# Another order of loads, scatters and VectorE's work in the up half of a fused projection and expert feed-forward kernel

## The reference

```python
ys = y * scale
d = rsqrt(einsum('bi,io->bo', ys * ys, weight * weight) + EPS)
xf = einsum('bsi,io->bso', x * ys[:, None, :], weight) * d[:, None, :]     # 512 -> 512
top1 = argmax(softmax(xf @ gate_w.T))                                       # 2 experts
masked = xf[None] * one_hot(top1, 2).T[:, :, None]
h = relu(einsum('end,edh->enh', masked, w1) + b1[:, None, :])               # 512 -> 2048
routing_output = (einsum('enh,ehd->end', h, w2) + b2[:, None, :]).sum(axis=0)
shared = relu(xf @ sw1 + sb1) @ sw2 + sb2                                   # 512 -> 2048 -> 512
out = x + routing_output + shared
```

## Time and profile before

| | |
|---|---|
| Time, median of 3 runs | 1463.98 us (1463.56 to 1464.52) |
| Time of the profiled execution | 1463.63 us |
| Its span in the profile | 1460.7 us |
| TensorE's mean granted clock | 0.993 |
| TensorE busy (matmuls) | 1425.5 us, 98% |
| TensorE, weight loads | 1175.8 us, 80% |
| VectorE busy | 847.2 us, 58% |
| ScalarE busy | 501.4 us, 34% |
| GpSimd busy | 314.4 us, 22% |
| HBM traffic over the span | 149 GB/s |

### The profile page before, as it was taken

How to read it: one execution, slowest core, us unless ns; L and a number is a source line. 1 busy time by engine, 2 the same in 40 slices (tenths; PEclk the granted TensorE clock), 3 DMA queues, 4 the chain that set the end, 5 groups by cost and what they waited for, 6 DMA issues and landing times.

```text
span 1460.7 us, 17708 instructions
## 1 busy us (share of the span) xinstructions
PE 1425.5 (98%) x6262; PEld 1175.8 (80%) x6262; DVE 847.2 (58%) x1362; ACT 501.4 (34%) x776; POOL 314.4 (22%) x354
## 2 busy tenths in 40 slices
PE   9997999999999999999999999999999999999998
PEld 8776778877877888888888888888888888888886
DVE  7895887857777878777864514224245532423235
ACT  4453553535454444444533211111123221111112
POOL 0000000062132110000023240614215151340533
PEclk9999899999999999999999999999999999999999
DMA  6947548494778898977675220312106231120312
GB/s 207 248 159 201 216 177 238 167 260 173 242 263 279 277 298 261 287 256 233 214 214 169 60 50 11 66 20 47 39 14 201 60 62 26 29 57 2 66 22 33
DMA packets 157190, 215.66 MB, mean 148 GB/s; under 512 B 46560, under 2 KB 67552, under 8 KB 157120
## 3 DMA queue, kind: packets, MB, share of 16 engines
q1 hardware_dynamic: 142240, 186.71, 39.9%
q0 software_dynamic: 14880, 28.07, 9.4%
HBM read 131.19 MB, written 85.75 MB: 149 GB/s over the span
## 4 chain that ended last, share of the span: by engine, by line
PE 75%; DVE 2%; issue 1%; DMA 1%; POOL 0%; ACT 0%; SPq 0%; another core or an unknown queue 0%; POOLq 0%; DVEq 0%; ACTq 0%
PE bank L1965 24%; PE bank L1989 23%; PE bank L1930 20%; PE bank L1893 8%; PE bank L1985 0%; DMA hin<-hidden_scratch 0%; DVE xw L1281 0%; DVE vb L1351 0%; DMA hidden_scratch<-vb 0%; POOL out L766 0%; DVE vt L1327 0%; DVE vb L1333 0%; DVE hl L1312 0%; DMA out<-res,tab 0%
## 5 line engine op out<-in xcount | busy, mean ns | idle before, releaser
L1893 PE MATMUL bank<-xw,w_hi 128*128 128x512 f32 x896 | 281.6, 396 | 22.5 <-DVE vb L1351 16.0
L749 POOL DMA_INDIRECT rows_e<-xf_scratch,soft x144 | 145.1, 1007 | 663.5 <-PE bank L1930 265.1
L1694 DVE CAST h_hi<-hf 128x512 fp32r<-128x512 f32 (+1 forms) x128 | 56.9, 445 | 387.3 <-ACT hf L1073 329.5
L1930 PE MATMUL bank<-hl,w_hi 128*128 128x512 f32 x896 | 277.3, 391 | 3.4 <-DVE hl L1312 3.3
L1073 ACT ACTIVATE hf<-bank,b 128x512 f32<-128x512 f32 (+1 forms) x128 | 87.4, 683 | 545.9 <-PE bank L1965 426.2
L1893 PEld LDWEIGHTS bank<-xw,w_hi 128*128 128x128 f32 x896 | 170.1, 191 | 62.6 <-DVE vb L1351 17.5
L1930 PEld LDWEIGHTS bank<-hl,w_hi 128*128 128x128 f32 x896 | 168.8, 189 | 39.6 <-DVE hl L1312 4.7
L1965 PE MATMUL bank<-xe_lo,w_hi 128*128 128x512 f32 (+1 forms) x512 | 197.7, 386 | 0.0
L1965 PE MATMUL bank<-xe_hi,w_hi 128*128 128x512 f32 (+1 forms) x512 | 197.6, 386 | 0.0
L1965 PE MATMUL bank<-xe_hi,w_lo 128*128 128x512 f32 (+1 forms) x512 | 196.0, 386 | 0.0
L1989 PE MATMUL bank<-w_lo,h_hi 128*128 128x512 f32 x496 | 193.0, 389 | 0.0
(11 more groups left out here) (216 smaller groups left out, 1699.3 us busy)
## 6 DMA issues: line engine op xcount, KB each, us to landing
hin<-hidden_scratch SPq DMA_DIRECT2D x112, 512.0 KB
hidden_scratch<-vb SPq DMA_DIRECT2D x80, 512.0 KB
hidden_scratch<-vt SPq DMA_DIRECT2D x32, 512.0 KB
stage<-w_pack SPq DMA_DIRECT2D x64, 256.0 KB
ring<-x_cols SPq DMA_DIRECT2D x32, 256.0 KB, 4.0
xf_scratch<-xo SPq DMA_DIRECT2D x32, 256.0 KB, 3.7
raw<-w_shared SPq DMA_DIRECT2D x32, 256.0 KB, 4.3
rows<-xf_scratch SPq DMA_DIRECT2D x16, 512.0 KB
```

The costliest lines, as they stand in the source:

```text
L749: pool.indirect_dma_start(rows_e[:, c % JN, :], None, xf_dram, bass.IndirectOffsetOnAxis(tab_rows[:, c:c + 1], 0)).then_inc(rows_gathered, ...
L1694: nc.vector.tensor_copy(h_hi[:, buf, 0:filled_n], hf[:, j % 2, 0:filled_n]).then_inc(hh_ready, 4)
L1893: last = nc.tensor.matmul(up_bank(u, UP_BANK[c])[p][:], w[:, DOWN_W[c], pair, part], xw[:, c, x, k, :], start=(c in FRESH and n == 1), sto ...
L1930: last = nc.tensor.matmul(bank[p][:], w[:, DOWN_W[c], i, part], hl[:, n % HL, h, :], start=(i == 0 and q == 0), stop=(i == PAIRS - 1 and q ...
```

## The change

The diff changes, in the order of the engines:

- **Projection.** The sums of weight job 1 move from tile 16 to 15, its high and low parts from 17 to 16; those of job 2 leave the projection for group 0. The first block's split and sums are spread over more tiles, one operation each.
- **SyncE.** The loads of weight jobs 3 to 7 leave its queue. Jobs 8 to 15 get seven buffers in place of four, and the loads of jobs 8 to 11 all stand in group 12 (before: 8 and 9 in group 12, 10 and 11 in group 13). The four quarters of the next block's `rows` are spread over groups `g` = 0, 1 and 2 of a block (before all four at `g` = 1). The first three hidden loads move from the start of group 15 to the end of group 14, and wait for other semaphores.
- **GpSimd** issues the loads of weight jobs 3 to 7, each after the job before has been split. Its 32 scatters start at the same group but come at 2 bank ends each (before 7/8); the table reads start at group 14 (before 12) and are spread.
- **VectorE.** `make_t4(u - 1)` stands first in a group, before the weight job's sums. The second weight job's sums stand after the adds of `vb11`. The flips stand at the end of the third group of a block, after `make_t3` (before at the start, after the last `make_t3`), and so do `slots` and `places` in theirs. The block change runs in the natural order of steps, with its sums in smaller pieces.
- **ScalarE.** At a block change one cast (`block_hi(s + 1, 1)`) comes before the take of `vt1`; the relu of `vb11` comes earlier; in the last group the first casts of hidden units come later.

```diff
-RAW_AT = (13, 17)
-SUMS_AT = (12, 16, 23)
+RAW_AT = (13, 16)
+SUMS_AT = (12, 15)
 FLIP_AT = (18, 19, 20, 21)
-X_AT = (22, 24, 26, 28, 30)
+X_HI_AT = (21, 24, 26, 27, 29)
+X_LO_AT = (22, 25, 27, 28, 30)
+X_SUM_AT = (23, 24, 26, 29)
 ...
-TABLE_GROUP = 12
+TABLE_GROUP = 14
 ...
-RAW_FIRST = {0: (4,), 1: (6,), 12: (8, 9), 13: (10, 11), 14: (12, 13)}
-RAW_SECOND = {0: (3,), 1: (5,), 2: (7,)}
+RAW_FIRST = {12: (8, 9, 10, 11), 14: (12, 13)}
+ROWS_BEFORE = {1: 1, 2: 3}
+ROWS_AFTER = {0: 0, 1: 2}
 RAW_LAST = 2 * PAIRS - 2
-RAW_KB = (208, 196, 160, 164)
-RAW_HOME = (0, 0, 0, 0, 0, 0, 0, 0, 0, 1, 0, 1, 0, 1, 2, 3)
+RAW_KB = (208, 184, 188, 192, 196, 160, 164)
+RAW_HOME = (0, 0, 0, 0, 0, 0, 0, 0, 1, 2, 3, 4, 0, 4, 5, 6)
 ...
                 if n == PAIRS:
+                    sp.wait_ge(xw_lo, STEPS * BLOCKS)
 ...
-            def next_rows(s):
+            def next_rows(s, q):
                 sp.wait_ge(xw_lo, STEPS * (s + 1))
-                for q in range(QD):
-                    sp.dma_start(rows[q * B32:(q + 1) * B32, :, :], quad_rows(q, s + 1)).then_inc(rows_in, DMA)
+                sp.dma_start(rows[q * B32:(q + 1) * B32, :, :], quad_rows(q, s + 1)).then_inc(rows_in, DMA)
 ...
-                if n == 0:
-                    sp.wait_ge(xw_lo, STEPS * BLOCKS)
-                if n == 3:
-                    sp.wait_ge(raw_ready, RAW_LAST)
-                    sp.wait_ge(sums_made, 4 * RAW_LAST)
+                if n < LOADS:
+                    in_place = max(m for m in range(2 * PAIRS) if RAW_KB[RAW_HOME[m]] == 184 + 4 * n)
+                    sp.wait_ge(raw_ready, in_place + 1)
+                    sp.wait_ge(sums_made, 4 * (in_place + 1))
 ...
-                    if last:
-                        for n in range(LOADS - 1):
-                            hidden_load(n)
                     if u > 0:
                         keep_t3(u - 1)
-                    if g == 1 and s < BLOCKS - 1:
-                        next_rows(s)
-                    for n in RAW_SECOND.get(u, ()):
-                        raw_load(n)
+                    if g in ROWS_BEFORE and s < BLOCKS - 1:
+                        next_rows(s, ROWS_BEFORE[g])
 ...
+                    if g in ROWS_AFTER and s < BLOCKS - 1:
+                        next_rows(s, ROWS_AFTER[g])
                     for n in RAW_FIRST.get(u, ()):
                         raw_load(n)
+                    if u == GROUPS * BLOCKS - 2:
+                        for n in range(LOADS - 1):
+                            hidden_load(n)
 ...
+            for n in range(len(LOAD_AT), PAIRS):
+                pool.wait_ge(raw_ready, n)
+                for h in range(2):
+                    src = w_shared[0, n + PAIRS * h].rearrange("p (q n) -> p q n", q=2)
+                    pool.dma_start(raws[0][:, h:4:2, :], src).then_inc(raw_late_in, DMA)
 ...
-                pool.wait_ge(up_mm, PER_GROUP * SCATTER_GROUP + c * 7 // 8)
+                pool.wait_ge(up_mm, PER_GROUP * SCATTER_GROUP + 2 * c)
 ...
+                    pool.wait_ge(up_mm, PER_GROUP * TABLE_GROUP + 5 * i)
 ...
-                if last:
-                    first_units(0, 2)
+                if more:
+                    block_hi(s + 1, 1)
                 wait(act, t1_out, DMA * u)
                 take(vt1, 2, 0, ACT.Identity)
                 if more:
-                    block_hi(s + 1, 1)
                     block_hi(s + 1, 2)
+                    block_hi(s + 1, 3)
+                if last:
+                    first_units(0, 2)
+                act.wait_ge(up_added, 6 * u + 2)
+                nc.scalar.activation(vb11[u % 2][:], vb11[u % 2][:], ACT.Relu).then_inc(b11_made, 1)
                 for n in jobs[1:]:
                     raw_hi(n)
+                if more:
+                    block_hi(s + 1, 4)
                 if last:
                     first_units(2, 4)
-                act.wait_ge(up_added, 6 * u + 2)
-                nc.scalar.activation(vb11[u % 2][:], vb11[u % 2][:], ACT.Relu).then_inc(b11_made, 1)
-                if more:
-                    block_hi(s + 1, 3)
+                act.wait_ge(up_added, 6 * u + 4)
+                nc.scalar.activation(vb22[:], vb22[:], ACT.Relu).then_inc(b22_made, 1)
                 for n in jobs[1:]:
                     raw_sums_hi(n)
                 if last:
                     first_units(4, 6)
-                act.wait_ge(up_added, 6 * u + 4)
-                nc.scalar.activation(vb22[:], vb22[:], ACT.Relu).then_inc(b22_made, 1)
-                if more:
-                    block_hi(s + 1, 4)
-                if last:
-                    first_units(6, HL)
                 if u == 0:
                     for i in range(RING):
                         act.wait_ge(xf_out[i], DMA * NT // RING)
                 wait(act, t4_out, DMA * u)
                 take(vb21, 6, 1, ACT.Relu)
+                if last:
+                    first_units(6, HL)
 ...
+                if u > 0:
+                    make_t4(u - 1)
+                for n in jobs[:1]:
+                    if n > 1:
+                        raw_sums(n)
                 if g == 0:
                     for i in range(X_EARLY, STEPS):
                         block_lo(s, i)
-                if g == 2 and s < BLOCKS - 1:
-                    for i in range(FLIPS):
-                        flip(s + 1, i)
                 for n in jobs[:1]:
-                    if n > 2:
-                        raw_sums(n)
                     raw_lo(n)
                     raw_sums_lo(n)
                 if u == CHOOSE_GROUP:
                     choose()
                 if u == RANK_GROUP:
                     count()
-                    slots()
-                if u == PLACE_GROUP:
-                    places()
-                if u > 0:
-                    make_t4(u - 1)
+                if more:
+                    block_lo(s + 1, 0)
+                    x_sum_of(s + 1, 0)
+                    x_sum_of(s + 1, 1)
+                    block_lo(s + 1, 1)
+                    x_sum_of(s + 1, 2)
+                add(vb11[u % 2], 3, 0, 0)
+                if more:
+                    block_lo(s + 1, 2)
+                add(vb11[u % 2], 3, 0, 1)
                 for n in jobs[1:]:
                     raw_sums(n)
-                if more:
-                    block_lo(s + 1, 0)
-                    x_sums(s + 1, 0)
-                    block_lo(s + 1, 1)
-                    x_sums(s + 1, 1)
-                if last:
-                    units_lo(0, 2)
-                add(vb11[u % 2], 3, 0, 0)
-                add(vb11[u % 2], 3, 0, 1)
+                add(vb22, 4, 2, 0)
                 for n in jobs[1:]:
                     raw_lo(n)
-                add(vb22, 4, 2, 0)
-                if more:
-                    block_lo(s + 1, 2)
-                    x_sums(s + 1, 2)
                 add(vb22, 4, 2, 1)
                 if more:
                     block_lo(s + 1, 3)
+                    x_sum_of(s + 1, 3)
+                if last:
+                    units_lo(0, 2)
+                add(vt1, 5, 4, 0)
+                add(vt1, 5, 4, 1)
                 for n in jobs[1:]:
                     raw_sums_lo(n)
-                add(vt1, 5, 4, 0)
-                add(vt1, 5, 4, 1)
                 if more:
                     block_lo(s + 1, 4)
                 if u == 0:
@@ -1405,15 +1413,23 @@
                     units_lo(2, 4)
                 make_t1(u)
                 if last:
+                    units_lo(4, 5)
                     raw_sums(RAW_LAST)
                     raw_lo(RAW_LAST)
-                    units_lo(4, 6)
+                    units_lo(5, 6)
                 make_t2(u)
                 if last:
                     raw_sums(RAW_LAST + 1)
                     raw_lo(RAW_LAST + 1)
                     units_lo(6, HL)
                 make_t3(u)
+                if g == 2 and s < BLOCKS - 1:
+                    for i in range(FLIPS):
+                        flip(s + 1, i)
+                if u == RANK_GROUP:
+                    slots()
+                if u == PLACE_GROUP:
+                    places()
```

More of the change, by code:

```diff
@@ L85 @@
 PER_GROUP = 2 * STEPS
-X_ORDER = (0, 1, 3, 2, 4, 5, 6)
-X_DONE = tuple(X_ORDER.index(c) + 1 for c in range(STEPS))
 X_EARLY = 5
@@ L290, in build @@
         raw_in = [sem(f"raw_in{i}") for i in range(len(RAW_KB))]
+        raw_late_in = sem("raw_late_in")
         rows_in = sem("rows_in")
```

47 lines of the change are left out of this document (26 added, 21 removed).

## The result

The changed kernel took 1480.5 us (median of 4 runs, 1479.3 to 1480.7) against 1463.8 for the kernel before (4 runs, 1462.3 to 1464.5): ratio 1.0114, 95% interval 1.0096 to 1.0131. It is slower, as forecast, but by 16.7 us where 7.5 had been forecast, and 0.5 us outside the range. In a later session the ratio was 1.0145 (1.0120 to 1.0171); there the kernel before took 1459.4, so times are compared only within a session. Losses by stage are compared across sessions; those of the kernel before come from one profile, of a run of 1463.6 us.

The account below looks back on a forecast made before the run. TensorE is busy in 98% of the span, so only its waits and lower clock count. Savings and new stops summed to +7.45 us on the profiled 1463.63, giving 1471 us, range 1452 to 1480.

Parts of the forecast that it names:

- What bounds the kernel: Whole kernel: TensorE is busy in 98% of the span, so only its waits and its lower clock gain or lose time.
- `make_t4` first: Groups 1, 2, 13 to 15: sums wait behind `make_t4` for the `vb21` write, stopping TensorE; group 13 +8.8 us.
- T - 5.3: Step 4 of a group: TensorE's stop in us, T being the time from group start to the start of `make_t4`.
- The step that failed: Group 15: `make_t4` starts 13.1 us in, stop 7.8, +4.1 us; with the down half's -3.3, together +0.8.
- the 239 GB/s that I used for group 13: Group 13: rate at which 1 MB of added raw loads takes 4.4 us ahead of the writes; 3.4 was taken.
- this row of the table: Group 15 and start of the down half: forecast change +0.8 us, measured +8.0.
- The clock: Behind TensorE's stops: 1.7 us charged for every new stop of 3 us or more, nothing below.
- Start of the down half: Start of the down half: loses 2.4 us in place of 5.7, -3.3, with the first hidden units there earlier.
- Group 14: Group 14: no load ahead of its write, `make_t4` starting about 6 us into the group, +0.7 us.
- Group 1 and group 10: Group 1: -7.8 us with group 0, its 12.8 us loss gone. Group 10: -4.7 us, `rows` loads blamed.
- the scatters as a rival of 0.1: Group 10: scatters lasting 87 us instead of 38 keep the 4.7 us loss, giving 1475.7 us; chance 0.1.
- Projection and flips: Projection: +3.0 us, sums one tile earlier block longer. Flips ahead of `make_t4`: group 3 +3.4, groups 7 and 11 +1.3 each.

Follow-up runs that it names:

- Experiment 1: The changed kernel with `make_t4(u - 1)` put back behind the group's first weight job: 1454.95 us, ratio to the kernel before 0.9977.
- experiment 7: The kernel before with only `make_t4(u - 1)` moved to be VectorE's first operation of a group: 1488.9 us in one run.
- Experiment 2: The changed kernel with the first three hidden loads put back to the start of group 15: 1474.4 us, ratio to the kernel before 1.0115.
- experiment 8: The changed kernel with `make_t4` behind the first weight job, hidden loads in group 15, and job 1's sums and parts at tiles 16 and 17: 1449.5 us.
- experiment 9: The kernel of experiment 8 with `make_t4` behind the next block's first two sums at a block change: ratio to the kernel before 0.9928.
- experiment 12: The kernel of experiment 9 with both adds of `vb22` ahead of the second weight job's sums: 1445.9 us, ratio to the kernel before 0.9889.
- experiment 6: The kernel before with only the loads of weight jobs 3 to 7 issued from GpSimd's queue: ratio to the kernel before 0.9976.
- experiment 11: The changed kernel with the four `rows` loads together at the start of a block's second group, as before: 1480.0 us in one run.
- experiment 10: The changed kernel with GpSimd's scatters at 7/8 bank ends each, as before: 1492.1 us in one run.
- Experiment 4: The changed kernel with job 1's sums back at tile 16 and its parts at tile 17 of the projection: 1475.4 us in one run.

## Why the prediction was wrong

**What bounds the kernel.** Right: the stops of TensorE and the half clock behind them add up to 16.9 us of the 16.8 that the spans differ by.

**`make_t4` first.** Right in mechanism and in the law. The stop at step 4 was to be T - 5.3; T of 9.1, 9.0, 12.0, 7.9 and 16.3 in groups 1, 2, 13, 14 and 15 gives 3.8, 3.7, 6.7, 2.6 and 11.0, and by exactly that much do the starts of TensorE's matmuls around step 4 stand further apart than the pitch of 0.2267 us. Experiment 1 removed it with one line, experiment 7 brought it into the kernel before.

**The step that failed** is group 15's: "raw loads and three hidden loads (3.48 us of issue, 1.5 MB) ahead: T = 11.5 + 1.6 = 13.1", with the down half "together +0.8". The mechanism was right and the term 1.6 for the hidden loads was too small; the prediction gives no working for it. Before, no hidden load stood ahead of group 15's write of `vb21`: the write was issued at 417.04 and the loads at 418.49. The change put all three ahead of it, and T went from 11.5 to 16.3: 4.8 us where 1.6 was forecast. The write is issued 5.6 us into the group instead of 2.8, and lands in 10.7 us instead of 8.6. Experiment 2, which undid that alone, gave 4.7 of T and 5.5 us of group 15 back. At the 239 GB/s that I used for group 13, 1.5 MB are 6.6 us; with that term in place of 1.6 the sum would have been about 12.5 us. Of the 7.2 us by which this row of the table was missed, T is about 3.2, the clock 1.2 and the start of the down half 2.9.

**The clock.** I charged 1.7 us for every stop of 3 us or more. That was right for stops of 3.7 us (groups 1 and 2: 5.5 lost, 3.7 or 3.8 of it standing). Behind the stops of 6.7 and 11.0 us it was 3.0 and 2.9: the clock stood at 0.50 for 13.5 us of group 15, 7.7 of it within the stop and the rest after it. The kernel before showed this already: group 1 lost 12.8 us by a stop of 10.1. That is 1.3 and 1.2 us in groups 13 and 15. The limit of 3 us does not hold either: TensorE stopped 2.6 us in group 3 and in group 14, and the clock fell behind the first (4.4 us lost) and not behind the second (2.8); in experiment 1 group 4 stopped 2.2 us and lost 3.9, in experiment 2 group 1 stopped 3.5 and lost 3.9. So the length of a stop alone does not tell whether it costs clock.

**Start of the down half.** I had 3.3 us come back there; 0.4 did, and in the second profile of the same kernel 2.0 more were lost. That the earlier hidden loads pay is not shown: in experiment 2, without them, it lost 6.9, in experiment 1, with them, 8.6. In experiments 8, 9 and 12, in which group 15 loses least (2.3, 0.3 and 0.0 us), the start of the down half loses 8.4, 9.9 and 9.0. Why is open.

**Group 14.** T was 7.9, not 6: the write of `vb21` was issued 1.9 us into the group and took 6.0 us to land, with nothing but the writes of `vt1` and `vt2` ahead of it in SyncE's queue and a read of GpSimd's table beside it. What slowed it was not tried.

**Group 1 and group 10.** Right in size, partly wrong in cause. Group 1's saving came only in part from the queue (3.3 of it, experiment 6); with `rows` together again 5.4 us of it are gone (experiment 11). For group 10 I blamed the `rows` loads and costed the paced scatters at nothing, with the scatters as a rival of 0.1 that would keep the loss because they last longer; in truth pacing them is what removed it (experiments 10 and 11).

**Projection and flips.** +3.2 for a forecast of +3.0, and +1.5 for +2.3. Experiment 4 confirms the cause of the first; the flips were not undone alone.
